# Column sums of the FFN activations taken in one run after the FFN, and the output transposed in bf16

## What is computed

```python
def _L0_attn_ref(x, Wq, Wk, Wv, Wo):
    ...
    q = apply_rope(q)
    k = apply_rope(k)
    ...
    scores = jnp.einsum('bshd,bstd->bsht', q, k) / jnp.sqrt(jnp.asarray(Dh, x.dtype))
    probs = jax.nn.softmax(scores, axis=-1)
    attn = jnp.einsum('bsht,bstd->bshd', probs, v).reshape(B, S, H * Dh)
    return attn @ Wo.T

def _L0_ffn_ref(x, wq_gate, s_gate, wq_up, s_up, wq_down, s_down):
    ...
    def _qlinear(x, wq, scale):
        W = (wq.astype(jnp.float32) - ZERO_POINT) * scale[:, None]
        return jnp.einsum('bsd,hd->bsh', x, W)
    gate = _qlinear(x, wq_gate, s_gate)
    gate = jax.nn.silu(gate)
    up = _qlinear(x, wq_up, s_up)
    return _qlinear(gate * up, wq_down, s_down)

xn = _layernorm(x, axis=-1)
x = x + _L0_attn_ref(xn, ...) + _L0_ffn_ref(xn, ...)
```

## Time and profile before

| | us |
|---|---|
| runs shown | 3142.64 and 3634.13, median 3388.38 |
| the profiled execution | 3143.68 |
| its span on the slowest core | 3142.1 |
| spans of the 8 cores | 3132.4 to 3142.1 |
| mean granted TensorE clock | 0.964 to 0.970 of full speed |

### The profile page before, as it was taken

One profiled execution on the slowest core, in us unless ns is written; L12 is line 12 of the kernel. 1 busy time (PEld: TensorE's weight loads), 2 busy tenths in 40 slices (PEclk: granted clock), 3 DMA queues, 4 the chain that ended last, 5 costly groups with the idle time before them and its releaser, 6 DMA issues.

```text
span 3142.1 us, 34496 instructions; the slowest of 8 cores (3132.4 to 3142.1 us)
## 1 busy us (share of the span) xinstructions
PE 2989.8 (95%) x14327; PEld 1381.4 (44%) x14327; DVE 459.2 (15%) x1021; ACT 489.5 (16%) x749; POOL 159.6 (5%) x306
## 2 busy tenths in 40 slices
PE   4999999999999989999949999999999999899998
PEld 2444454444444434444424444544444444344443
DVE  3001070000000011111130101700000000111111
ACT  3000072111111100000040001721111111000000
POOL 0000000000000001001000000000000000011010
PEclk9999979999999999999969999699999999999999
DMA  5221201212121144464462222011212121444634
GB/s 136 81 81 67 81 15 54 81 67 81 67 81 67 68 173 144 151 234 143 173 147 72 76 81 77 5 67 67 81 67 81 67 79 69 173 151 150 236 140 155
DMA packets 50072, 321.14 MB, mean 102 GB/s; under 512 B 5817, under 2 KB 5872, under 8 KB 22272
## 3 DMA queue, kind: packets, MB, share of 16 engines
q0 software_dynamic: 42816, 268.59, 24.2%
q1 hardware_dynamic: 4672, 33.56, 3.5%
q10 hardware_dynamic: 2432, 16.78, 2.0%
HBM read 209.85 MB, written 16.78 MB: 72 GB/s over the span
## 4 chain that ended last, share of the span: by engine, by line
PE 92%; ACT 2%; DMA 2%; DVE 2%; issue 1%; ACTq 0%; DVEq 0%; POOL 0%; SPq 0%; POOLq 0%
PE p L620 39%; PE p L429 21%; PE p L754 19%; PE p L738 7%; PE pb L602 1%; ACT xn_b L334 1%; DMA xbuf<-x 1%; PE pb L705 1%; DMA dwst<-wd 1%; PE pb L471 1%; PE p L522 1%; PE pb L529 1%; DVE rs L556 0%; PE p L491 0%; PE p L517 0%
## 5 line engine op out<-in xcount | busy, mean ns | idle before, releaser
L620 PE MATMUL p<-xnT,wst 128*128 128x512 bf16 x5632 | 1232.8, 380 | 0.0
L620 PEld LDWEIGHTS p<-xnT,wst 128*128 128x128 bf16 x5632 | 544.9, 98 | 682.7 <-issue 39.4
L429 PE MATMUL p<-xnT,wst 128*128 128x512 bf16 x3072 | 665.9, 380 | 0.0
L754 PE MATMUL p<-actT,dwst 128*128 128x512 bf16 x2816 | 623.8, 381 | 6.1 <-DMA dwst<-wd 6.0
L429 PEld LDWEIGHTS p<-xnT,wst 128*128 128x128 bf16 x3072 | 301.3, 98 | 363.8 <-issue 3.2
L754 PEld LDWEIGHTS p<-actT,dwst 128*128 128x128 bf16 x2816 | 276.6, 98 | 342.9 <-issue 20.1
L640 DVE TENSOR_TENSOR actT<-gate_b,up_b 128x512 bf16<-128x512 bf16 x176 | 74.8, 425 | 1201.1 <-ACT up_b L635 1201.1
L738 PE MATMUL p<-attnT,wst 128*128 128x512 bf16 x1024 | 239.4, 388 | 3.2 <-DMA wst<-wo 3.2
L629 ACT ACTIVATE gate_b<-p,sgT 128x512 bf16<-128x512 f32 x176 | 120.9, 687 | 542.4 <-PE p L620 542.4
L635 ACT ACTIVATE up_b<-p,suT 128x512 bf16<-128x512 f32 x176 | 120.9, 687 | 474.7 <-PE p L620 474.7
L738 PEld LDWEIGHTS p<-attnT,wst 128*128 128x128 bf16 x1024 | 101.9, 100 | 118.5 <-issue 19.5
(11 more groups left out here) (71 smaller groups left out, 844.9 us busy)
## 6 DMA issues: line engine op xcount, KB each, us to landing
wst<-wgu POOLq DMA_DIRECT2D x88, 1024.0 KB, 4.9
dwst<-wd POOLq DMA_DIRECT2D x128, 704.0 KB, 4.1
wst<-wo POOLq DMA_DIRECT2D x32, 1024.0 KB, 6.4
wst<-wq POOLq DMA_DIRECT2D x16, 1024.0 KB, 5.1
wst<-wk POOLq DMA_DIRECT2D x16, 1024.0 KB, 5.1
wst<-wv POOLq DMA_DIRECT2D x16, 1024.0 KB, 5.1
out_nat<-x SPq DMA_DIRECT2D x4, 4096.0 KB, 18.8
y<-out_nat SPq DMA_DIRECT2D x8, 1024.0 KB, 9.1
```

The costliest lines, as they stand in the source:

```text
L429: e.matmul(o, s, r, start=stt, stop=sp),
L620: e.matmul(o, s, r, start=stt, stop=sp),
L754: e.matmul(o, s, r, start=stt, stop=sp),
```

## The change

- `colsum_step` and what followed it in `ffn_phase` go. `out_phase` now begins with a call of the existing `colsum` over `actT`, in bank `p0`. For the first half there are 44 matmuls, a cast, a subtraction and the small DMA; then the same for the second half. The first matmul waits for the last product L640 (`act_done`). The matmuls of the second half wait for the subtraction of the first, since they write the same bank.
- The number of column-sum matmuls is the same: 88 for each chunk.
- `outT0` and `outT1` become BF16 and move to other bytes of the same scratch area. The 256 transposes of the output take bf16 data and the bf16 identity and write bf16 into `pb4` and `pb5`. DVE adds bf16 from PSUM to `out_nat` in place of F32.

```diff
-    outT0 = at("outT0", [128, 512], F32, A0 + 11264)
-    outT1 = at("outT1", [128, 512], F32, A0 + 13312)
+    outT0 = at("outT0", [128, 512], BF16, A0 + 14336)
+    outT1 = at("outT1", [128, 512], BF16, A0 + 15360)
...
-            if hb >= 2:
-                colsum_step(hb - 2)
-        for hbp in range(HCN - 2, HCN):
-            colsum_step(hbp)
...
-            th = P.add("vector",
...
-            tl = P.add("vector",
...
-            td = P.add("sync",
...
-        return mx(*mult_toks), mx(*hilo_toks)
+        return mx(*mult_toks)
...
-    def out_phase(c, act_done, hilo2, attn_done):
+    def out_phase(c, act_done, attn_done):
+        hilo2 = colsum(act_done, hilo_ac,
+                       lambda k, tb: actT[:, k * 1024 + tb * 512: k * 1024 + tb * 512 + 512],
+                       HCN, p0,
+                       war=mx(st_["actT_read"] if c > 0 else None))
...
-                                 e.transpose(o, s, eye_f[:]),
+                                 e.transpose(o, s, eye_b[:]),
...
-                pv3 = tp.rearrange("p (j cc) -> p j cc", j=4)
+                pv3 = tp[:, 0:512].rearrange("p (j cc) -> p j cc", j=4)
...
-                pend[0] = (ot, pf4 if oc % 2 == 0 else pf5,
+                pend[0] = (ot, pb4 if oc % 2 == 0 else pb5,
```

## The result

The changed kernel takes 3113.3 us in the median of its executions, against 3144.8 us for the kernel before on the same chip: a ratio of 0.9901, with a 95% interval of 0.989 to 0.9913. That is 31.5 us, or 1.0%, less. The forecast was 3115 us.

A forecast was written before the change was run, and what follows sets the result against it. The prediction took PE, busy 95% of the span, as the bound. Pairs removed, way to Wo and transposes summed as -46.8 + 31.1 - 12.8 = -28.5 us against 3143.7 us, giving 3115 us, range 3103 to 3140.

The forecast's parts named there:

- What bounds the kernel: Whole kernel: PE, busy 95% of the span; a change pays where it shortens PE's list or removes its idle time.
- The pairs removed: Between FFN blocks: 41 column-sum pairs a chunk at 0.57 us leave PE's list, 46.8 us less in all.
- The way from the FFN to Wo: FFN's last matmul to Wo's first: 27.1 us a chunk, 54.2 us for both against 23.1, so +31.1 us.
- The restart: Wo's first matmuls after the 3.5 us stop: the same slow restart at half clock as before, no gain counted.
- The transposes: Output phase: four bf16 transposes take 0.24 us instead of 0.44, 0.20 us for each of 64 groups, 12.8 us less.
- What I put at nothing in the output phases: Output phases: nothing counted for the moved load of x into `out_nat`, nor for DVE's operations on bf16.
- Rival 1: Column-sum run: the clock falls to half, 0.427 us a matmul, 37 us for all 176, 3152 us; chance 0.15.
- Rival 2: Output phase: the transposes gain nothing, since the type doesn't set their 0.44 us; 3128 us; chance 0.06.
- Rival 3: Between FFN and Wo: the small DMAs stay in the open, 5 us more a chunk, 3125 us; chance 0.03.
- Rival 4: FFN: without the pairs it is throttled to clock 0.81, +282 us, 3397 us; chance 0.02.

The follow-up runs named there:

- e7: The changed kernel with the two small matmuls that spread the correction moved behind the first output block's matmuls; 3103.6 and 3104.7 us.
- e3: The kernel before, with column sums in runs of eight after every fourth FFN block instead of pairs after each; ratio 0.9937 to the kernel before.
- e4: The kernel before, with 128 columns of ones instead of one as the column sums' stationary operand; 3126.0 us in one execution.
- e2: The kernel before, with only outT and its transposes made bf16, column sums left between FFN blocks; ratio 0.9952 to the kernel before.
- e1: The changed kernel with outT and its transposes left in F32, so only the column sums are moved; 3124.9 us in one execution.
- e5: The changed kernel with 128 columns of -128 as stationary operand and a bank per half, giving the correction directly; ratio 0.9845 to the kernel before.
- e8: The changed kernel with a bank for each half of the column sums; 3104.9 and 3106.1 us.

## Why the prediction was right, step by step

- **What bounds the kernel.** PE's list. Right: every experiment that shortened it or took a stop out of it was paid, e7 only in part, and 86 additions a chunk on DVE cost nothing that can be seen.
- **The pairs removed.** The mechanism was right, the term too small: -46.8 us against -51.3 measured (25.9 and 25.4). The step that failed is the price of a dense matmul, 0.2167 us, which I took from QKV's 332.81 us. QKV starts behind the normalization with six matmuls 0.427 us apart, and they are in that mean. Between FFN blocks it is 0.2158 us, so a pair costs 14.44 - 64 x 0.2158 = 0.63 us and not 0.57. I also had no cause for the part of it that isn't columns; e3 and e4 show it.
- **The way from the FFN to Wo.** Forecast 27.1 us, measured 1110.03 - 1083.07 = 27.0 us in chunk 1 and 2659.50 - 2632.24 = 27.3 us in chunk 2, from the end of the FFN's last matmul in the chain. The stops were forecast at 1.5, about 1.7 and 3.5 us and measured at 1.57, 1.72 and 3.48 us in chunk 1. This sum held as each duration had its row at the same place before.
- **The restart.** Expected as slow as before, and it is: Wo's 16 matmuls take 5.7 and 5.8 us in the two chunks against 5.3 and 6.2 us before. That a stop of 3.5 us is what does it was read off one row; e7 bears it out.
- **The transposes.** Forecast -12.8 us. The place in the list gave 0.215 us for each group, -13.8 us for 64, and e2 alone lies 12.7 us below before. On core 5 the two output phases together were only 9.0 us shorter, but cores 4 to 7 had short stretches at clock 0.81 in both profiles. Cores 0 to 3 had none: their output phases took 953.7 us in the mean before, and e2's eight cores, also without such stretches, 939.8. So the transposes gave all of it: 13.9 us.
- **What I put at nothing in the output phases.** Moving the sums costs some 3 us there. Cores 0 to 3 took 942.3 us in the changed kernel, 2.5 us more than e2, and e1's eight cores 957.2 us, 3.5 us more than cores 0 to 3 before. Of this 1 to 2 us are waits of PE for weights at the turn of the halves. Their mean over the eight cores was 9.4 us before, 10.8 us in the change (on core 5 9.2 and 12.3), 11.3 us in its second profile and 11.4 us in e1. The profiles with the sums still in the FFN (e2, e3, e4) have 9.2 to 10.3 us. So they come with the move; why they do, and what the rest is, no run shows. On core 5 this nearly cancels what I had missed in the FFN.
- **Rival 1, the clock in the run.** It didn't come: 1.00 over both runs, 0.216 us a matmul. One column at work kept the clock as well as 128 (e5).
- **Rival 2**, transposes that gain nothing, falls with e2. **Rival 3**, small DMAs in the open, falls too: the first half's DMA ran beside the second run, and one small DMA of 1.6 us is in the open.
- **Rival 4, a throttled FFN**, didn't come: the FFN's 609 us without a break stand at clock 1.00. The stretch of the table for them:

```profile
474.20:1083.00 608.80, 608.80 (x2816) 275.60 (x2814) 36.98 (x87) 122.13 (x177) 22.68 (x43) 1.00 0.21 75
```

The rule of the Trainium skill ("TensorE: Matmul & The Clock Gate", the note on the peak-current limiter in Part 1), weighed in the prediction, is not borne out by this row.

The time came out within 2 us of the forecast partly by luck: one term was 4.5 us too small and another gave 3.8 us less.

## What to carry to other kernels

When one engine's list is the bound, price a small piece of work by what it does to that list: its own time, the joins on both sides of it, and the stops that it opens. Work that is spread between other matmuls isn't free, work gathered at the end needs its tail hidden behind something else, and the best place may be another engine with idle time: here the change as a whole gave 1.0%, and with the additions on DVE in its place 2.7%. Take the price of a unit from the stretch where it will run, not from a mean that takes in a slow start.

## What the runs showed of the hardware that was not expected

- A one-column stationary operand among 128-column ones costs PE 0.20 us for each place, whether two or eight matmuls stand in it, since neither load is brought forward (0.42 and 0.44 us without a load at PEld). At full width the same matmuls cost only their 0.2158 us.
- An F32 transpose of 128x128 holds PE for 0.11 us, a bf16 one for 0.056 us (four in 0.44 and 0.22 us).
- Column sums with a single column kept the granted clock at 1.00, and 88 of them in a row (e8) ran at the same 0.216 us as full matmuls. A stop of 3.5 us behind them was enough for a restart at a mean granted clock of 0.60; with a stop of 1.78 us (e7) the restart was at full speed.
